# Taking a 48-partition stack of low-rank factors to all 128 partitions with zero rows, in a fused S4 and LoRA feed-forward kernel

## The reference

```python
xn = _layernorm(x, axis=-1)
s = _L0_attn_ref(xn, ...)      # one S4 kernel K of length 512, causal convolution along the row, + D * xn
h1 = xn @ w1.T + 2 * (xn @ A1.T) @ B1.T        # 512 -> 1376, rank 16
h3 = xn @ w3.T + 2 * (xn @ A3.T) @ B3.T
g  = silu(h1) * h3
f  = g @ w2.T + 2 * (g @ A2.T) @ B2.T          # 1376 -> 512, rank 16
x  = x + s * silu(f)
```

## Time and profile before

| what | value |
|---|---|
| median of 3 runs | 442.14 us (441.92 to 442.59) |
| profiled execution, from first to last instruction (span) | 439.7 us |
| PE busy | 429.8 us, 98% |
| DVE busy | 159.6 us, 36% |
| ACT busy | 100.2 us, 23% |
| POOL busy | 63.6 us, 14% |
| mean granted TensorE clock | 0.993 of full speed |

### The profile page before, as it was taken

How to read it: one execution, slowest core, us unless ns; L and a number is a source line. 1 busy time by engine, 2 the same in 40 slices (tenths; PEclk the granted TensorE clock), 3 DMA queues, 4 the chain that set the end, 5 groups by cost and what they waited for, 6 DMA issues and landing times.

```text
span 439.7 us, 5019 instructions
## 1 busy us (share of the span) xinstructions
PE 429.8 (98%) x1868; PEld 341.6 (78%) x1868; DVE 159.6 (36%) x245; ACT 100.2 (23%) x167; POOL 63.6 (14%) x127
## 2 busy tenths in 40 slices
PE   8979999999999999999999999999999999999995
PEld 8857777776777888888878888888878888888774
DVE  3537665554539432122224232132224211111114
ACT  3433332232223111122112111122112111111111
POOL 1326541621222011400000011400000000000000
PEclk9989999999999999999999999999999999999998
DMA  8493643222040610100001510100002000000002
GB/s 267 114 197 104 220 144 97 66 70 75 18 133 37 215 49 0 48 1 0 1 0 72 167 48 0 48 0 0 0 0 86 10 0 0 0 0 0 0 0 95
DMA packets 14063, 26.19 MB, mean 60 GB/s; under 512 B 2480, under 2 KB 4208, under 8 KB 14032
## 3 DMA queue, kind: packets, MB, share of 16 engines
q1 hardware_dynamic: 13888, 25.41, 19.3%
q0 software_dynamic: 160, 0.59, 0.4%
HBM read 20.37 MB, written 4.53 MB: 57 GB/s over the span
## 4 chain that ended last, share of the span: by engine, by line
PE 92%; DMA 3%; SPq 1%; DVE 1%; ACT 1%; POOL 1%; issue 1%; DVEq 0%
PE h L778 20%; PE h L779 19%; PE h L780 19%; PE f L778 10%; PE f L780 9%; PE f L779 9%; DMA lora_stack<-lora_spread_split 2%; PE spare L765 2%; DMA xn<-x_dram 1%; PE spare L760 1%; SPq L457 1%; PE spare L780 1%; PE spare L778 1%; PE spare L779 1%; PE spare L884 0%
## 5 line engine op out<-in xcount | busy, mean ns | idle before, releaser
L778 PE MATMUL h<-xt,w 128*128 (+4 forms) x356 | 140.5, 395 | 0.6 <-DVE w L621 0.6
L779 PE MATMUL h<-xt,w 128*128 (+4 forms) x356 | 138.2, 388 | 0.0
L780 PE MATMUL h<-xt,w 128*128 (+4 forms) x356 | 138.1, 388 | 0.0
L778 PEld LDWEIGHTS h<-xt,w 128*128 128x128 f32 (+1 forms) x356 | 66.4, 186 | 18.4 <-issue 1.8
L657 DVE TENSOR_TENSOR g<-g,h 128x512 f32<-128x512 f32 (+1 forms) x44 | 30.2, 687 | 132.7 <-PE h L780 132.7
L780 PEld LDWEIGHTS h<-xt,w 128*128 128x128 f32 (+1 forms) x356 | 66.3, 186 | 15.0
L779 PEld LDWEIGHTS h<-xt,w 128*128 128x128 f32 (+1 forms) x356 | 66.3, 186 | 14.2
L662 DVE TENSOR_TENSOR ghl<-g,ghl 128x512 fp32r<-128x512 f32 (+1 forms) x44 | 32.7, 742 | 104.5 <-ACT ghl L519 104.4
L778 PE MATMUL f<-ghl,w2f 128*128 128x512 f32 (+1 forms) x176 | 70.3, 399 | 0.0
L780 PE MATMUL f<-ghl,w2f 128*128 128x512 f32 (+1 forms) x176 | 69.5, 395 | 0.0
L779 PE MATMUL f<-ghl,w2f 128*128 128x512 f32 (+1 forms) x176 | 69.2, 393 | 0.0
(11 more groups left out here) (101 smaller groups left out, 270.8 us busy)
## 6 DMA issues: line engine op xcount, KB each, us to landing
raw<-w_dram SPq DMA_DIRECT2D x28, 256.0 KB, 3.4
xres<-xT_dram SPq DMA_DIRECT2D x4, 1024.0 KB, 7.2
outT_dram<-xres SPq DMA_DIRECT2D x16, 256.0 KB, 2.4
rows_next<-x_dram SPq DMA_DIRECT2D x4, 512.0 KB, 3.5
scale_rows<-scales_scratch SPq DMA_DIRECT2D x3, 512.0 KB, 3.8
xn<-x_dram SPq DMA_DIRECT2D x4, 256.0 KB, 4.3
rows<-x_dram SPq DMA_DIRECT2D x2, 512.0 KB, 7.1
raw<-w_dram SPq DMA_DIRECT2D x4, 224.0 KB, 2.5
```

What stands on the lines that cost most here:

```text
L778: pe.matmul(out, w[1], m[0], start=start, stop=False)
L779: pe.matmul(out, w[0], m[1], start=False, stop=False)
L780: return pe.matmul(out, w[0], m[0], start=False, stop=stop)
```

## The change

`lora_stack` becomes a tile of 128 partitions with the same columns. Its instructions on PE thereby have a contraction of 128 in place of 48; their number, columns and order are the same. Rows 48 to 127 must hold zeros, so the whole tile is zeroed ahead of the six DMAs: ACT copies a column of zeros into the moving half (3264 columns) right after its first `silu`, and POOL's memset fills the other half (2400 columns) as its first work. SP waits for both, next to `spread_lo`.

```diff
-        lst = put("lora_stack", [len(STACK) * R, LORA_COLS], F32R)
+        lst = put("lora_stack", [P, LORA_COLS], F32R)
...
-        spread_in, stack_in = sem("spread_in"), sem("stack_in")
+        spread_in, stack_in, stack_cleared = sem("spread_in"), sem("stack_in"), sem("stack_cleared")
...
             sync.wait_ge(spread_lo, 1)
+            sync.wait_ge(stack_cleared, 2)
             for n, (st, mv) in enumerate(STACK):
...
             nc.scalar.activation(g[:, P:P + 1], g[:, 0:1], ACT.Silu).then_inc(table_loaded, 1)
+
+            nc.scalar.copy(lst[:, ST_COLS:LORA_COLS], g[:, 0:1].to_broadcast([P, MV_COLS])).then_inc(stack_cleared, 1)
             rows_norm(0)
...
+            nc.gpsimd.memset(lst[:, 0:ST_COLS].bitcast(F32), 0.0).then_inc(stack_cleared, 1)
             pool.wait_ge(const_in, 16)
             for r in range(0, RT, 2):
                 rows_rstd(0, r)
```

## The result

| | before | after |
|---|---|---|
| median of 4 runs each | 442.03 us (441.41 to 442.59) | 434.06 us (433.76 to 434.59) |
| ratio, 95% interval | | 0.9821 (0.9804 to 0.9838) |
| profiled execution, span | 439.7 us | 432.3 us |
| PE busy | 429.8 us, 98% | 420.8 us, 97% |
| mean granted TensorE clock | 0.993 | 0.994 |

What follows compares the result with a forecast made beforehand. PE was taken as the bound, with 92% of the chain. 8.0 + 0.15 + 0.19 - 0.05 = 8.3 us off 442.14 us gave 433.8 us; own bounds 432.6 to 434.6, 8-in-10 range 432.3 to 437.0 us.

Steps and rivals of the forecast that it cites:

- the 48 rows: At PE's folds from the stack: 48 rows beside neighbours' 128 make each place cost 0.38 us more than its columns.
- (a): Folds with 128 rows: 21 places from 46 us on lose their passage excess, 21 x 0.38 = 8.0 us.
- (b): Four places before 46 us: 0.15 us from the first three, 0.19 us at the fourth, where DVE binds PE.
- (c, d): Start of program: ACT's copy (3.6 us) and POOL's memset (3.8 us, 5.7 at most) hidden in idle time, cost nothing.
- a sign: Check in the changed profile: POOL's first statistics should still start at 6.57 us; a slipped start means the prediction is wrong.
- (e): SP's second wait before the stack's DMAs: met on arrival, 0.05 us allowed on the chain.
- Both hold: DVE's low part for gate of j=5 (2.3 us ahead) and POOL's coefficients for `krow` (5.0 us) keep up with PE.
- a sign of being wrong: Check in the changed profile: new idle time of PE behind DVE or POOL after 46 us would refute the prediction.
- The distance of 2.4 us between median and span: Whole kernel: the runs' median lies 2.4 us above the profiled span of 439.7 us, a difference taken as fixed.

Runs made afterwards that it cites:

- Experiments 1 to 4: Against the kernel before: 128 partitions cleared but 48 read, 442.68 us; 64 rows, 442.66 us; 72 rows, 434.88 us; changed kernel with only w2 folds at 48, 437.33 us.
- experiment 5: The kernel before, unchanged, profiled once more as a control for the program's start; span 440.9 us.
- experiment 1: Stack of 128 partitions with all clears and waits, but PE's folds read 48 rows, against the kernel before: 442.68 us, ratio 0.9995.

## Why the prediction was right

**The cause.** The forecast rested on the 48 rows, judged from the folds of 16 rows and the transposes of 128. Experiments 1 to 4 show it: the same reads at 48 or 64 rows pay, at 72 or 128 they don't, and the price goes with each single passage. How many folds stand between the two passages doesn't matter: at the second place, with six fold matmuls, the steps from 35.00 to 36.54 took 1.54 us before, and from 35.34 to 36.48 they take 1.14 us after, 0.40 us less, as at a place with one or two. "TensorEngine Tiling (Array Packing)" of the Trainium skill, Key Properties, has the mode switch that drains TensorE; its list of modes under Available Configurations (32, 64 and 128 rows) fits the border that the runs found between 64 and 72. No run shows the mode itself, only the idle time and the border. "TensorE: Matmul & The Clock Gate" of the Trainium skill, Why this matters for your kernels, says that a single matmul of K=32 takes as long as one of K=128. The trace agrees at 48 rows only where no passage lies in front: a fold of w2 right behind another fold took 394 ns, as with 128 rows, and the others 492 ns (medians and least values of L760 and L763).

**The size (a).** Predicted were 0.38 us for each of 21 places, 8.0 us. From the fold at 46.62 to the last at 122.39 the kernel before takes 75.77 us (experiment 5), the kernel after takes 114.83 - 46.21 = 68.62 us: 7.15 us for 20 places, 0.36 us each, 7.5 us for 21. At the passage itself the gain is 0.39 us (1.08 against 0.69 us), 7.8 us for 20 places, so 0.65 us of it is lost between them. One part is a new wait of PE, 0.33 us (below). The other lies inside the stages: ten steps of an up stage took 55.96 - 53.69 = 2.27 us before, and 55.01 - 52.70 = 2.31 us after. The new steps of 0.231 us are close to the 0.233 us of stages without folds, so it is the kernel before that ran them short behind a passage; why, I can't say. The price of 0.38 us was read at the passage alone and set against steps of 0.233 us; read from stage to stage it was less. So this term was too large by 0.5 us.

**The early places (b).** Predicted: PE bound by DVE's add at the fourth place, 0.15 and 0.19 us gained. The mechanism came as predicted: the stall at 43.13 is there, released by DVE. A second stall, of 0.27 us at 39.53, was not forecast. From the first fold to the fifth place the kernel before takes 46.62 - 30.73 = 15.89 us (experiment 5) and the kernel after 46.21 - 30.70 = 15.51 us, 0.38 us less; 0.19 us of it is the entry of the fifth place, which the sum had among the 21. Forecast for the stretch by the same count: 0.53 us, so the early places gave 0.19 us of the 0.34 us.

**The clears (c, d).** Both were hidden, as predicted. The memset took 2.10 us (3.8 us estimated, 5.7 at the most) and the copy 2.89 us (3.6 estimated): both were mis-sized on the safe side. POOL's first statistics came at 7.14 instead of the 6.57 that I had named as a sign, but the memset had ended at 2.85, and the kernel before, profiled again, has them at 7.01: this varies with the arrival of the rows.

**SP's wait (e)** was allowed 0.05 us; nothing shows (experiment 1, 0.9995 with an interval of 0.13% to either side).

**The others' pace.** "Both hold" was true of the two couplings that the prediction looked at, but there was a closer one. PE has one new idle time after 46 us, which the prediction had named as a sign of being wrong. From the timeline of the kernel after:

```profile
107.34 1.73 DVE L624 TENSOR_TENSOR w<-raw,w 128x448 fp32r<-128x448 f32 x1
...
108.61 0.40 PE L783 MATMUL h<-xt,w 128*128 128x512 f32 x1
...
109.17 0.47 PE L781 MATMUL h<-xt,w 128*128 128x512 f32 x1 [0.16 <-DVE w L624]
```

The step is 0.56 us in place of 0.23: PE waits for a low part of DVE that takes 1.73 us. The kernel before shows how near this was, in its timeline of PEld, where the weight load for the same stage already waited for the same low part, though PE itself did not:

```profile
116.13 0.19 PEld L778 LDWEIGHTS h<-xt,w 128*128 128x128 f32 x1 [0.18 <-DVE w L621]
```

The loss of 0.33 us is small, and it is contained in the 7.15 us of (a).

**The sum.** By measured parts it is 7.5 + 0.2 = 7.7 us against 8.3 us predicted; the runs say 8.0 us with an interval of 7.2 to 8.7 us. With 7.7 us the forecast would have been 434.4 us. That 433.8 us lies only 0.3 us from the median is partly luck: the interval covers both sums, and terms (a) and (b) were both too large. The span was forecast worse, 431.4 us against 432.3. The distance of 2.4 us between median and span was not fixed; it is 1.8 us after, and the kernel before, profiled again, had a span of 440.9 us where its first profile had 439.7.

## What to carry to other kernels

A matmul of few rows among full ones costs little itself, but going in and coming out each cost about 0.19 us at the upper clock, since the next weights aren't loaded early; here 72 rows were enough to avoid it, 64 were not. To find such places, look for weight loads that start with their own matmul after an idle time that no engine ended, then compare steps from start to start, and over whole stages too, since the passage alone gave too high a price here. Before counting every place, ask who frees what it needs: the first four places gave almost nothing, because DVE's add held the bank. And look for loads that already wait a little for another engine: that is where a faster PE stands still next.

## What the runs showed of the hardware

After 3.6 us in which PE waited for the stack, the granted clock was mostly at 1.2 GHz, and it stayed at 2.4 GHz when 15 matmuls filled this time (0.54 against 1.00 in the windows above). How long the lower level lasts after the wait differs between profiles with the same start: in the kernel after it was all but over by 34.2 us (0.96 from there to 36.4), but in the kernel with 64 rows the two windows up to 36.4 us are both at 0.50:

```profile
30.50:34.20 3.70, 3.70 (x10) 3.04 (x11) 0.69 (x1) 1.79 (x4) 0.00 (x0) 0.50 0.87 327
34.20:36.40 2.20, 2.20 (x7) 1.65 (x5) 0.00 (x0) 0.68 (x2) 1.36 (x2) 0.50 0.00 0
```

By estimate the last 2.2 us at half speed cost 1.1 us. The profiles show about as much: from the first fold to the fifth place the kernel with 64 rows takes 47.84 - 30.50 = 17.34 us and that of experiment 1, whose clock is back at 0.91 in the second window, 46.56 - 30.66 = 15.90 us. The kernel with 72 rows has 0.50 in both windows too. This may be one reason why single runs of a kernel differ by 1 us; only one run of each has a trace, so that is not shown.
